# Block 2 of a two-block convolution kernel recut into a front and a back stage, with borders cleared by ScalarE and softmax denominators inverted before they are spread

## The reference, cut to what matters

```
# block 1, per image: single-head attention over 1024 pixels on 48 of 192 channels
xn   = layernorm(x[:48]);  q, k, v = bn(w_qkv @ xn)         # 16, 16, 48 channels
attn = softmax(q.T @ k / 4);  out = v @ attn.T
y    = bn(w_proj @ relu(concat(out, x[48:])))
# block 2, per image
q, k, v = qkv(x)                                            # attention over channels, 8 heads of 24
attn = softmax(l2norm(q) @ l2norm(k).T * temperature);  at = attn @ v
conv_x = dw3x3(conv1x1(v))                                  # depthwise 3 x 3
t    = conv1x1(at, 192 -> 32);  ci1 = conv1x1(mean(t))
ci2  = conv1x1(dw7x7_dil3(dw3x3(t)));  channel_map = conv1x1(t * ci1 * ci2)
s1, s2 = split(dw3x3(conv1x1(conv_x, 192 -> 96)));  spatial_map = conv1x1(gelu(s1) * s2)
y    = proj(at' * sigmoid(spatial_map) + conv_x * sigmoid(mean(channel_map)))   # at' = at + channel_map
```

## Time and profile before

| | |
|---|---|
| device time, median of 3 runs | 431.94 us (430.26 to 434.22) |
| device time of the profiled execution | 430.68 us |
| its span, first to last instruction | 428.9 us |
| mean granted TensorE clock | 0.926 of full speed |
| DMA | 12.34 MB, mean 29 GB/s |

### The profile page before, as it was taken

The page is one execution under the profiler, slowest core; times in us unless marked ns, Lnnn a source line. Parts: engine busy times, 40 slices in busy tenths (PEclk is TensorE's granted clock), DMA queues, the critical chain, the costliest instruction groups (busy, mean ns, idle before and its releaser), DMA issues. The chain is left out here.

```text
span 428.9 us, 4998 instructions
## 1 busy us (share of the span) xinstructions
PE 356.4 (83%) x1996; PEld 174.2 (41%) x1996; DVE 287.5 (67%) x490; ACT 157.3 (37%) x255; POOL 35.7 (8%) x45
## 2 busy tenths in 40 slices
PE   0649787989697898996978889887999887998996
PEld 0425443323255743331433454423345474444331
DVE  5637657447494589914542998678548878799464
ACT  1212252543602254472122731472262354443340
POOL 2102060002002100000101006000000001000000
PEclk9999998999997588899989996989999998798999
DMA  8530000000000012000002000030000003221004
GB/s 233 164 100 0 2 0 0 2 0 1 0 2 0 2 26 59 0 2 0 0 0 75 0 1 2 0 73 12 2 0 2 0 2 99 59 56 30 0 0 147
DMA packets 6067, 12.34 MB, mean 29 GB/s; under 512 B 2078, under 2 KB 2718, under 8 KB 5918
## 3 DMA queue, kind: packets, MB, share of 16 engines
q1 hardware_dynamic: 5532, 11.97, 10.5%
q10 hardware_dynamic: 514, 0.08, 0.1%
HBM read 5.32 MB, written 3.15 MB: 20 GB/s over the span
## 5 line engine op out<-in xcount | busy, mean ns | idle before, releaser
L1473 DVE SCALAR_TENSOR_TENSOR cx<-cpA,dw2w,cx 128x1024 f32<-128x1024 f32 x32 | 40.9, 1278 | 6.2 <-ACT cx L1946 6.1
L1484 DVE SCALAR_TENSOR_TENSOR dd<-spp,wt,dd 112x1024 f32<-112x1024 f32 x32 | 41.1, 1284 | 2.0 <-ACT dd L2032 1.1
L586 PE MATMUL psO<-pT,vt 128*64 128x512 f32 x96 | 29.6, 698 | 2.4 <-ACT pT L1916 2.2
L1473 DVE SCALAR_TENSOR_TENSOR cx<-cpB,dw2w,cx 128x512 f32<-128x512 f32 x32 | 23.9, 746 | 0.8 <-ACT cx L1946 0.8
L762 PE MATMUL psR<-up,wb 128*32 128x256 f32 (+1 forms) x336 | 23.5, 430 | 0.8 <-DMA up<-up 0.8
L2249 POOL TENSOR_TENSOR gr<-gvar,mhalf 128x2 f32<-128x2 f32 x8 | 6.0, 753 | 189.3 <-DVE gvar L1283 189.3
L1328 DVE TENSOR_REDUCE nm<-psB 128x1 f32<-128x1024 f32 x16 | 19.5, 1217 | 0.5 <-PE psB L556 0.4
L1340 DVE RECIPROCAL rb<-psA 112x512 f32<-112x512 f32 x3 | 10.1, 3355 | 13.0 <-PE psA L595 13.0
L1264 DVE BATCH_NORM_STATS2 st<-x 128x6 f32<-128x512 f32 x24 | 15.6, 685 | 3.6 <-DMA x<-x_dram 3.3
L1328 DVE TENSOR_REDUCE nm<-psA 128x1 f32<-128x1024 f32 x12 | 14.6, 1219 | 3.7 <-PE psA L556 3.7
L1916 ACT ACTIVATE pT<-psA 128x1024 f32<-128x1024 f32 x12 | 12.3, 1022 | 12.9 <-PE psA L576 12.9
(11 more groups left out here) (480 smaller groups left out, 768.4 us busy)
## 6 DMA issues: line engine op xcount, KB each, us to landing
up<-up SPq DMA_DIRECT2D x12, 200.0 KB, 3.1
x<-x_dram SPq DMA_DIRECT2D x4, 512.0 KB, 7.2
out_dram<-x SPq DMA_DIRECT2D x8, 256.0 KB, 2.1
wt<-params_dram SPq DMA_DIRECT2D x1, 1151.5 KB, 9.9
tp<-tp SPq DMA_DIRECT2D x8, 136.0 KB, 2.4
x<-x_dram SPq DMA_DIRECT2D x8, 128.0 KB, 5.7
out_dram<-x SPq DMA_DIRECT2D x8, 128.0 KB, 2.4
wt<-params_dram SPq DMA_DIRECT2D x1, 213.5 KB, 3.3
```

The costliest lines, as they stand in the source:

```text
L586: last = mm(s.o_ps[rows(n), :], s.vt[:, t, :], s.pT[t % 2][:, n * HB:(n + 1) * HB], start=(t == 0), stop=(t == NKT - 1))
L1473: v.scalar_tensor_tensor(acc, img, dw2w[:, blk, tap:tap + 1], acc, ALU.mult, ALU.add).then_inc(cv_s.of(c), 1)
L1484: v.scalar_tensor_tensor(acc, t.spp[:, dy:dy + HH, dx:dx + WW], par("w_spdw")[:, tap:tap + 1], acc, ALU.mult, ALU.add).then_inc(dv_s.of(c), 1)
```

## The change

**Stages.** Block 2 is split. The front stage of an image (`conv1`, its `conv2` steps, and the channel attention down to `t_weights`) has one tile set and the two banks of psB, for all four images in turn. The back stage (`t_product` and everything behind it) keeps two sets with psR/psS and psA/psO. Three small tiles and `X`, `cx` that go from front to back exist twice (`pair[c % 2]`). `conv1_a(c)` now waits for the front stage of image c - 1, and `t_product` and `sp_in` wait for the last `result` on their back set. Images go in the order 0, 1, 2, 3.

**Score tiles.** Since psB is given away, `score_rows` of images 2 and 3 and `scores_t` of images 1 to 3 have one two-bank tile, psA. `score_rows(b, t)` then waits for `row_max(b, t - 1)`, and `scores_t(b, t)` for `exps(b, t - 1)`; q and k of images 2 and 3 share psA too, so the k product waits for `q_low`.

**Denominators.** They come out as 128 x 8 with 8 short matmuls, are inverted in that form and then spread by `denominator_rows`, as the layer norm's factors are; `attn_relu` reads them from PSUM.

**Clearing.** POOL's 16 `fill`s go. ACT clears the borders alone, in 8 + 9 + 9 instructions (`zero_front`, `zero_back`), an activation with scale 0.

**Lists.** All five are written anew; `setup2_e` moves from ahead of `q_low(1)` to behind `split_max(1)` on DVE; 11 calls of `keep_warm` (a matmul of 256 columns whose result nobody reads) stand in PE's list up to the first scores; on SP `store(1)` stands ahead of `shift_t(2)`.

```
+SLOTF, TURNF = (0, 0, 0, 0), (0, 1, 2, 3)
+            t.F = [psB[:, 0:HB], psB[:, HB:N]]
-        one[0].score_ps, one[1].score_ps = (psR, psB), (psA, psB)
-        one[0].scoreT_ps, one[1].scoreT_ps = (psR, psR), (psA, psB)
+        score_ps = [(psR, psB), (psA, psB), (psA, psA), (psA, psA)]
+        one[0].scoreT_ps, one[1].scoreT_ps = psR, psA
...
             def score_rows(b, t):
-                if t >= 2:
-                    pe.wait_ge(*nm_s(b, t - 1))
+                behind = 2 if b < 2 else 1
+                if t >= behind:
+                    pe.wait_ge(*nm_s(b, t + 1 - behind))
...
             def denominators(b):
-                for n in range(2):
-                    last = mm(s.den_ps[rows(n), :], par("pick_den")[:, n:n + 1].broadcast_to([SPN + 1, SP2]),
-                              s.osb[0:SPN + 1, :], start=True, stop=True)
+                for t in range(4):
+                    last = mm(s.den_ps[:, 2 * t:2 * t + 2], s.osb[0:SPN + 1, t * P:(t + 1) * P], par("pick_den"),
+                              start=True, stop=True)
+            def denominator_rows(b):
+                pe.wait_ge(*dr_s(b, 1))
+                spread(s, s.row_ps).then_inc(db_s.of(b), 1)
             def inverse_denominators(b):
-                v.reciprocal(s.rb[:], s.den_ps[0:SPN, :]).then_inc(dr_s.of(b), 1)
+                v.reciprocal(s.rT[:], s.den_ps[:, 0:NKT]).then_inc(dr_s.of(b), 1)
...
             def conv1_a(c):
-                if TURN2[c]:
-                    pe.wait_ge(*oo_s(c - 1, 3))
+                if c == 0:
+                    pe.wait_ge(s_zf, n_zf)
+                    pe.wait_ge(*nm_s(1, NKT))
+                else:
+                    pe.wait_ge(*mce_s(c - 1, 3))
+                    pe.wait_ge(*mte_s(c - 1, 4))
             def t_product(c):
+                pe.wait_ge(s_zb[SLOT2[c]], n_zb)
+                if TURN2[c]:
+                    pe.wait_ge(*oo_s(c - 1, 3))
...
+            def zero(o, done):
+                a(o, one_col.broadcast_to(list(o.shape)), ID, scale=0.0).then_inc(done, 1)
-            def fill(i, k):
-                g.memset(tile[:], 0.0).then_inc(s_fill, 1)
```

More of the change, by code:

```diff
@@ L263, in build @@
[L263 to L268, removed]
-        one[0].score_ps, one[1].score_ps = (psR, psB), (psA, psB)
-        one[0].scoreT_ps, one[1].scoreT_ps = (psR, psR), (psA, psB)
-        one[0].q_ps, one[1].q_ps = psR, psB
-        one[0].k_ps, one[1].k_ps = psA, psA
+        one, back = [], []
+        with ExitStack() as early:
+            one.append(block1_tiles(0, early))
@@ new lines, in build @@
+        front = front_tiles()
+        back.append(back_tiles(0))
+        with ExitStack() as early:
+            one.append(block1_tiles(1, early))
+        back.append(back_tiles(1))
+        padded_tiles(1, back[1])
+        padded_tiles(0, back[0])
+        front.cpA = sb("cpA", [P, PW, PW])
+        front.cpB = sb("cpB", [P, BH, PW])
+        pair = [pair_tiles(i) for i in range(2)]
+        score_ps = [(psR, psB), (psA, psB), (psA, psA), (psA, psA)]
+        q_ps = [psR, psB, psA, psA]
+        k_ps = psA
@@ L427, in _ @@
             shift_u(1)
-            shift_t(3)
             store(1)
-            shift_u(3)
             shift_t(2)
             shift_u(2)
+            shift_t(3)
+            shift_u(3)
+            store(2)
             store(3)
-            store(2)
-            sp.wait_ge(s_out, 16 * 4 * B)
+            for b in range(B):
+                sp.wait_ge(s_out[b], 16 * 4)
         @block.tensor
@@ L1666, in _ @@
             merge(0, 2)
+            block1_out(2, 0)
+            channel_stats(1, 2, 0)
+            channel_stats(1, 2, 1)
+            block1_out(2, 1)
+            conv2(1, 15)
+            channel_stats(1, 2, 2)
+            moments(1, 2)
+            result(0, 0)
+            result(0, 1)
+            result(0, 2)
+            group_stats(1, 2)
+            copy_wma(1)
             group_shift(1, 2)
@@ L1986, in copy_wmt @@
+                a(pair[c % 2].wmtB[:, 0:P], front.F[1][:, C:C + P], ACT.Copy).then_inc(mte_s.of(c), 1)
                 for n in range(2):
-                    a(t.wmtB[rows(n), P + n * CB:P + (n + 1) * CB], t.R[0][rows(n), C + P:2 * C],
+                    a(pair[c % 2].wmtB[rows(n), P + n * CB:P + (n + 1) * CB], front.F[1][rows(n), C + P:2 * C],
                       ACT.Copy).then_inc(mte_s.of(c), 1)
             def pad_t(c):
-                t = two[SLOT2[c]]
+                t = back[SLOT2[c]]
```

1227 lines of the change are left out of this document (623 added, 604 removed).

## The result

| | before | after |
|---|---|---|
| device time, median (range) | 432.06 us (430.26 to 434.22) | 394.22 us (394.12 to 395.88) |
| ratio, 95% interval | | 0.9131 (0.9083 to 0.918) |
| span of the profiled execution | 428.9 us | 393.8 us |
| time of that execution | 430.68 us | 395.88 us |

The account below looks back on a forecast made before the run. PE work (83% busy) plus the gaps in which PE waits bound the kernel. Start 32.0 plus 315.3 of PE work at share 0.87 (362.4) gave span 394.4, time 396.2, median 397; range 380 to 420.

Parts of the forecast that it names:

- Sum: Whole kernel: start 32.0 plus the rest 362.4 gives span 394.4, time 396.2; forecast of the median 397.
- Start: Up to the first row maximum: 2.6 from earlier `layer_norm(0)`, 2.6 if `keep_warm` lifts PE's pace; 37.2 becomes 32.0.
- Share: PE busy time times clock over length, after the start: from 0.794 to 0.87, with PE work 315.3 us.
- Stages: Three strands side by side after the start: most of the gain, through useful share 0.87, giving 362.4 us.
- Denominators: Chain from denominators to multiply: 4.44 to 2.31 us, less handoffs 2.0 per image, 8.0 in all.
- the mark of 2.3 us: Sign for the denominators: 2.3 us from the end of `attn_out` to the multiply's operands.
- Clearing: Two DVE operations stretched beside POOL's clearing fall to about 0.17 and 0.43: 5.2 us, both on chains.
- One-bank rhythm: Images' score tiles: row maxima 2.04 apart, exponentials 1.85; 14.6 and 4.3 us if bare, hidden by other work.
- the second rival: One-bank scores: PE and DVE each wait behind the other's fill, 438 us; sign DVE idle over 15 us; chance 0.08.
- The first: Whole kernel: only the local savings arrive, useful share stays 0.794, time 418; chance 0.17.
- The third (clock): One-bank scores and exponentials of images 2 and 3: PE's clock falls to half, 27.0 us new, 424; chance 0.06.
- Stage marks: Signs for the stages: image 3's `block1_out` at 275 to 295, under 105 us behind it, useful share 0.85 or more.

Follow-up runs that it names:

- a_nokeep: Changed kernel without the 11 `keep_warm` products: 393.43 us, ratio 0.9078 to the kernel before.
- b_local: Kernel before with the new denominators, the border clearing on ScalarE and the start changes, none of the stages: 424.88 us, ratio 0.9765.
- a_fillout: Changed kernel with the work between the score tiles of images 2 and 3 put behind the last of them (PE and DVE lists): 429.15 us, ratio 0.9926.
- a_den: Changed kernel with the old denominators back (wide product, wide reciprocal, no spreading): 405.76 us, ratio 0.940 to the kernel before.
- b_den: Kernel before with the new denominators alone: 425.22 us, ratio 0.979.
- b_clear: Kernel before with POOL's 16 fills gone and 30 short border instructions on ScalarE: 430.99 us, ratio 0.9927.
- a_clear: Changed kernel with POOL clearing whole tiles again instead of ScalarE's 26 instructions: 398.28 us, ratio 0.9217 to the kernel before.
- b_one: Kernel before with one score tile instead of two (maxima of images 2 and 3, exponentials of 1 to 3): 461.06 us, ratio 1.0586.
- b_local2: Kernel before with the three local changes (denominators, clearing, start) but without `keep_warm`: 416.2, 423.0, 423.4 and 427.6 us, no interval.

## Why the prediction was right, step by step

- **Sum.** Predicted 32.0 + 362.4 = 394.4 of span, measured 33.95 + 359.85 = 393.8. The start came out 1.95 us longer and the rest 2.55 shorter, and inside the rest two misses cancel as well (under Share). That the sum is right to 1 us is luck; the range of 380 to 420 didn't need it. The sum also has no term for the 8.0 of the denominators and the 5.2 of the clearing: they lie inside the 0.87, which the prediction chose between two stretches and didn't derive.
- **Start.** `xn` of image 0 ends at 25.57 and not at 28.79, 3.2 us earlier. 2.7 of this is the statistics step, as forecast (2.6); 0.5 is that image 2's x is there at 24.29 and not at 24.82 in this execution (in `a_nokeep` it comes at 24.83, and `xn` ends at 26.12). The other 2.6, q, k and v at full pace, did not come (q product 2.02). The step that failed is "if they lift the pace": the first row maximum is at 33.95 and not near 32, and `a_nokeep` shows `keep_warm` to be worth nothing here.
- **Share.** 0.87 predicted, 310.1 / 359.85 = 0.862 measured. The work came out 5.2 us under the 315.3. That was an over-count in the prediction: from 38.45 to 46.4 us before, score tiles took 1.22, half pace, while the clock column said 1.00, so most of PE's 9.84 busy us from 37.2 to 50 counted double, 4.9 too much. Without them the first of the five stretches has the share (58.2 - 4.9) / 69.6 = 0.77 and not the 0.84 with which the first two rivals were weighed. In the time, the over-count is worth 5.2 / 0.87 = 6.0 us one way, and 0.862 instead of 0.87 is 3.4 us the other way. The stretch (columns as above), and one such tile in PE's order of time, both of before:

```profile
37.20:50.00 12.80, 9.84 (x23) 4.39 (x23) 11.03 (x20) 0.00 (x1) 3.07 (x4) 1.00 0.00 0
```

```profile
39.58 1.22 PE L556 MATMUL psB<-ks,qs 96*128 96x512 f32 x2
```

- **Stages.** "Here lies most of it" holds: `b_local` to after is 0.0634, 27 us, where the prediction had 21 (418 to 397). The local savings gave 10 where it had 14. `a_fillout` shows what the 27 us rest on: without the pieces of other stages in the gaps of the one score tile, all of them are gone. No run takes apart what else changed with the stages (the order of the images, the new lists elsewhere, SP's queue), so the 27 are the price of all that together.
- **Denominators.** The 8.0 us are 9 in the kernel before, and 6.3 to 11.6 in the changed one. From the start of the product to the multiply the changed kernel takes 2.7, 4.2, 6.1 and 2.5 us in images 0 to 3, because the lists put other PE and DVE work in between for images 1 and 2; the mark of 2.3 us is missed there. But against kernels that differ in this alone, the chain is shorter about as forecast: `a_den`, with the same lists, takes 4.5, 5.5, 8.3 and 4.5, which is 7.4 more in sum, and the kernel before takes 18.6 in sum where `b_den` takes 13.0, with spans 5.3 apart. In image 3, with 2.5 near the 2.41 predicted, PE and then DVE read, in order of time:

```profile
290.40 1.05 PE L624 MATMUL psA<-wt,osb 113*128 113x2 f32 x8
291.75 1.09 PE L544 MATMUL psO<-wt,rT 128*64 128x128 f32 x16 [0.30 <-DVE rT L1386]
```

```profile
291.49 0.21 DVE L1386 RECIPROCAL rT<-psA 128x8 f32<-128x8 f32 x1 [1.44 <-PE psA L624]
292.89 1.40 DVE L1394 SCALAR_TENSOR_TENSOR xm<-osb,psO 48x512 f32<-48x512 f32 x2 [1.20 <-PE psO L544]
```

  The small reciprocal takes 0.21, where 0.17 was taken. For the 9 in `b_den` beside a chain of 5.6, the interval begins at 5.8; that DVE's 12.6 us of freed time, with `conv2` steps behind the reciprocal, gives the rest is argued, not shown.
- **Clearing.** No `dk` pair is over 0.45, as predicted. 5.2 was too much: `b_clear` gives 3 and `a_clear` 3.7, neither with a narrow interval. The copy of 2.57 (60.72 to 63.29 before) ran beside image 1's q product (60.85 to 61.95), for which DVE's next step waits anyway, so only part of it was on the path.
- **One-bank rhythm.** 2.04 and 1.85 were right: bare score tiles at full pace are 2.05 apart, and exponentials of image 3 follow at 279.46, 281.31, 283.16. That fill hides it was right too (`a_fillout`), but DVE is busy 74% in both images' scores, not over 90%; PE is the fuller one (86% and 97%). DVE's idle time in front of the 16 maxima is 10 us, under the 15 at which the second rival would act.
- **Rivals.** The first, built, has the ratio 0.9765, 422 beside 432, and not 418. The third (clock) didn't happen: 0.98 and 0.96 in the two stretches. It happens at once when the fill is gone: `a_fillout` 0.60, `b_one` 1.22 for a score tile. The Trainium skill's page "TensorE: Matmul & The Clock Gate", section "A second HAM failure mode: psum-queue depth-cycling", has PE's clock swing between full and half when PE idles briefly between groups of matmuls that go through PSUM banks in turn. The bare gaps agree with it (0.60). With fill, PE idles 2.8 of 20.55 us in image 2's scores and the clock is 1.00, as the prediction said "by the rows alone".
- **Stage marks.** `block1_out(3)` at 297.58 is outside the 275 to 295 that were named, and the 96.2 behind it within "under 105": the middle is fuller and slower than forecast, the end shorter. What is left there is half pace again (image 3's `conv1_a` at 308.20 takes 3.50, image 2's 1.98) and waits at the joins of the two last back stages, none over 1.8 us. The longest waits of PE in this stretch (who waited, for whom, us, times, longest):

```profile
PE psR L853 <- ACT th L2104: 1.8, 1, 1.8
PE psB L728 <- ACT attT L2041: 1.3, 1, 1.3
```

## What to carry to other kernels

Giving up a double buffer can pay when the bank buys a third strand of work, but only together with an order that puts that work into the gaps: the same kernel with bare gaps loses 34 of 38 us, and the old kernel with one bank is 25 us slower. To price such a change, take the useful share of the most comparable stretch, drained end included, and not that of the densest one: 0.85 was nearer to the measured 0.862 than 0.93. Check the pace by the duration of a known matmul, above all near the start, where the clock column can be wrong. Local savings measured one by one (9, 3 and 5 us) need not add up (10).

## What the runs showed of the hardware

- The granted clock of a stretch can read 1.00 while PE runs at its 1.2 GHz level. In the kernel before it reads 1.00 from the start up to 72 us, over the q product of 2.02 at 28.84 and the score tiles of 1.22 too; in the changed kernel it first falls at about 25 us. The misreadings found all lie ahead of a trace's first fall. Behind it, durations looked at agree with it: the q product of 2.02 at 132.22 lies where it reads 0.50. `b_local` and `b_local2` have the same products at the same double length from 50 to 61 us, and the column says 0.50 for one and 1.00 for the other:

```profile
51.00:62.40 11.40, 11.40 (x49) 7.49 (x49) 2.74 (x11) 3.63 (x6) 1.64 (x1) 0.50 0.00 0
```

```profile
50.00:61.00 11.00, 11.00 (x48) 7.10 (x47) 2.73 (x11) 3.64 (x6) 1.64 (x1) 1.00 0.00 0
```

- Gaps of 1.32 us between score tiles of 0.73 brought PE to half pace after two of them in image 2 of `a_fillout` and after one in image 3, and products that nobody reads in six of these gaps of image 2 kept it at full pace (0.82 for a score tile, clock 1.00).
- A cast of 1024 elements took 4.3 us longer (4.46 for 0.17) beside a row of POOL memsets.
- The 11 `keep_warm` products, nine of them ahead of image 0's q product, changed nothing at it: 2.02 with them and without. Full pace was there at 21.32 (1.09 for 1.98) and gone at 25.62, behind a wait of 1.81 us.
